# Splitting the 4-bit quantisation of one feed-forward block: eight chunks beside the first attention, three on GpSimd later

## What is computed

```python
x = x + tanh(g_xattn[0]) * L0_xattn(layernorm(x), ctx, ...)   # 32 heads of 128
x = x + tanh(g_ffn[0])   * L0_ffn(layernorm(x), 4-bit weights)
x = x + tanh(g_xattn[1]) * L1_xattn(...)
x = x + tanh(g_ffn[1])   * L1_ffn(...)     # base product + top-2 of 28 LoRA experts
x = x + tanh(g_xattn[2]) * L2_xattn(...)   # one head
x = x + tanh(g_ffn[2])   * L2_ffn(...)     # silu(x@dq1.T) * (x@dq2.T) @ dq3.T
x = x + tanh(g_xattn[3]) * L3_xattn(...)
x = x + tanh(g_ffn[3])   * L3_ffn(...)
```

```python
absmax = max(abs(block)); v = block / absmax
idx = searchsorted(bounds, v)          # 15 bounds, 16 code values
dq = CODE[idx] * absmax
```

## Time and profile before

| | us |
|---|---|
| median of 3 runs | 1882.26 |
| lowest, highest | 1872.6, 1884.25 |
| the profiled execution, its own time | 1874.59 |
| its span in the profile | 1872.9 |
| PE busy (share of the span) | 1460.5 (78%) |
| DVE busy | 1213.1 (65%) |
| ACT busy | 611.7 (33%) |
| POOL busy | 348.9 (19%) |
| mean granted PE clock | 0.889 |

### The profile page before, as it was taken

The page is one execution under the profiler, slowest core; times in us unless marked ns, Lnnn a source line. Parts: engine busy times, 40 slices in busy tenths (PEclk is TensorE's granted clock), DMA queues, the critical chain, the costliest instruction groups (busy, mean ns, idle before and its releaser), DMA issues.

```text
span 1872.9 us, 18291 instructions
## 1 busy us (share of the span) xinstructions
PE 1460.5 (78%) x6556; PEld 1020.8 (55%) x6556; DVE 1213.1 (65%) x1816; ACT 611.7 (33%) x912; POOL 348.9 (19%) x330
## 2 busy tenths in 40 slices
PE   7878778778746678578878888779999999997104
PEld 5545454445324545365746666557777777776101
DVE  4887888788885677542354444646666665667777
ACT  3544444444432233210121221134444344443003
POOL 1122132122213700010000000112212222123600
PEclk9998998989878799789569999989999999998556
DMA  5675776665572000002010112101101111000001
GB/s 193 156 181 137 143 178 150 160 141 138 117 136 99 34 11 1 0 23 68 0 34 17 46 38 77 48 9 57 57 23 39 53 57 57 1 1 1 0 0 45
DMA packets 37183, 127.69 MB, mean 68 GB/s; under 512 B 4288, under 2 KB 10304, under 8 KB 30896
## 3 DMA queue, kind: packets, MB, share of 16 engines
q1 hardware_dynamic: 26224, 83.38, 13.1%
q0 software_dynamic: 10880, 43.26, 13.0%
HBM read 72.63 MB, written 10.75 MB: 45 GB/s over the span
## 4 chain that ended last, share of the span: by engine, by line
PE 58%; DVE 20%; issue 10%; DVEq 5%; ACT 3%; POOL 1%; POOLq 1%; DMA 1%; SPq 0%
PE PS L151 10%; PE PS L153 9%; PE PS L152 9%; PE PS L492 6%; PE PS L467 4%; PE PS L825 3%; PE PS L861 3%; DVE AR L610 3%; DVE AR L2082 2%; DVEq L320 2%; DVE AR L631 2%; PE PS L451 2%; DVE AR L2076 2%; DVE AR L2080 1%; PE PS L847 1%
## 5 line engine op out<-in xcount | busy, mean ns | idle before, releaser
L492 PE MATMUL PS<-R,PT 128*128 128x512 f32 x256 | 158.0, 775 | 130.3 <-DVE X L646 130.3
L492 PEld LDWEIGHTS PS<-R,PT 128*128 128x128 f32 x256 | 61.5, 252 | 215.8 <-issue 215.8
L152 PE MATMUL PS<-R16r 128*128 128x512 f32 (+1 forms) x328 | 122.9, 375 | 0.0
L153 PE MATMUL PS<-R16r 128*128 128x512 f32 (+1 forms) x312 | 121.2, 388 | 0.0
L467 PE MATMUL PS<-R,HT 128*128 128x256 f32 x512 | 115.9, 379 | 0.0
L400 POOL DMA_DIRECT2D AR<-AR x40 | 49.6, 1240 | 307.7 <-DMA AR<-AR 239.4
L467 PEld LDWEIGHTS PS<-R,HT 128*128 128x128 f32 x512 | 94.8, 190 | 11.6
L151 PE MATMUL PS<-R16r,HTr 128*128 128x512 f32 (+1 forms) x224 | 91.3, 408 | 6.1 <-DVE X L1218 4.6
L151 PE MATMUL PS<-HTr,R16r 128*128 128x512 f32 (+1 forms) x240 | 90.4, 377 | 3.1 <-DVE R16r L193 1.6
L610 DVE SCALAR_TENSOR_TENSOR AR<-OT,AR 128x2112 f32<-128x2112 bf16 x32 | 75.5, 2359 | 21.8 <-ACT OT L555 19.4
L153 PE MATMUL PS<-HTr,R16r 128*128 128x512 f32 (+1 forms) x240 | 88.3, 368 | 0.0
(11 more groups left out here) (284 smaller groups left out, 3702.8 us busy)
## 6 DMA issues: line engine op xcount, KB each, us to landing
AR<-AR POOLq DMA_DIRECT2D x40, 1056.0 KB, 8.2
OR<-in_wo SPq DMA_DIRECT2D x12, 1024.0 KB, 5.0
dequantised<-AR SPq DMA_DIRECT2D x8, 1056.0 KB, 4.5
WR<-in_w0q SPq DMA_DIRECT2D x8, 1024.0 KB, 5.9
AR<-in_w3q SPq DMA_DIRECT2D x8, 1024.0 KB, 4.9
WR<-dequantised SPq DMA_DIRECT2D x22, 256.0 KB, 2.8
AR<-in_nf SPq DMA_DIRECT2D x4, 1056.0 KB, 6.0
nf_in<-in_nf SPq DMA_DIRECT2D x4, 1056.0 KB, 5.9
```

Source lines behind the costliest of these rows:

```text
L152: nc.tensor.matmul(out, ah, bl, start=False, stop=False)
L153: return nc.tensor.matmul(out, al, bh, start=False, stop=last_)
L492: i = nc.tensor.matmul(bank(5 + tt), PT[:, at:at + P], vo[:, pr, b, :], start=pr == 0, stop=pr == 1)
```

## The change

The chunks are cut anew. There are now eleven chunks of 128 x 1536 (`NF` = 11), one per slice of 128 hidden units, and the blocks of w3 are reordered so that slice f of stage f2 needs chunks up to f+1. Eight chunks stay beside stage x0, one per group as before, with the same instructions on 1536 columns. POOL's sum of `nf_above` and `nf_below` there becomes one more accumulating transfer (`join`), and the multiplication by the block maxima (`rescale`) is issued by POOL after the first accumulation of the next group. `nf_below`, `nf_above` and `absmax` have a buffer more. A chunk is stored by five transfers (six for chunk 0, seven for chunk 10) in place of one.

The last three chunks (8, 9, 10) are loaded once a1 is through with the buffers. DVE takes their maxima and normalises them in `dve_late`, between norm 3 and the gating of f1. POOL then computes all 15 steps of each: for each step it does one comparison with a multiplication (`tensor_scalar`) and, from the second on, one sum (`tensor_tensor`), both with a drain behind, and at the end the multiplication by the maxima and the stores, issued by POOL. Of the 45 steps five come after the gating (`h_ready`), twelve between norm 4 and norm 5, and 28 behind norm 5. The loads of slices 7, 8 and 9 in stage f2 wait for chunks 8, 9 and 10. A few semaphores of f3 are merged.

```diff
-NBU = NF * D // QB // NG
-NBT = 3 * NBU
+NBT = 3 * D // QB
+NARENA = 11616
@@ stores
+        def store_chunk(queue, k, src, signal):
+            queue.dma_start(scratch[:, 0:2, k * D:(k + 1) * D], src[:, 0:2 * D].rearrange("p (w n) -> p w n", w=2))\
+                .then_inc(signal, 16)
+            for at, b, n in w3_runs(k):
+                queue.dma_start(scratch[:, 2, b * QB:(b + n) * QB], src[:, 2 * D + at * QB:2 * D + (at + n) * QB])\
+                    .then_inc(signal, 16)
@@ pool_x0
-                nc.gpsimd.tensor_tensor(nf_result(g), nf_below, nf_above, ALU.add)
-                pool.drain().then_inc(A0["nf_free"], 1)
+                nc.gpsimd.dma_start(nf_below(g), nf_above(g), accum_op=ALU.add, max_dma_last_dim=4 * N_NF // 2)\
+                    .then_inc(A0["nf_joined"], 16)
+
+            def rescale(g):
+                pool.wait_ge(A0["nf_joined"], 16 * (g + 1))
...
+            for g in range(NG):
+                accumulate(g, 1)
+                if g:
+                    rescale(g - 1)
+                for k in range(2, NDOWN):
+                    accumulate(g, k)
+                join(g)
+            rescale(NG - 1)
@@ stage f1
+        def dve_late(dve):
+            dve.wait_ge(A0["nf_in"], 16 * ((NF + 1) // 2))
+            dve.wait_ge(A0["nf_in_odd"], 16 * (NF // 2))
+            for i, k in enumerate(LATE):
+                v = late_in(i).rearrange("p (n q) -> p n q", q=QB)
+                nc.vector.tensor_reduce(absmax[:, k], v, AX.X, ALU.max, apply_absolute_value=True)
...
+                nc.vector.tensor_tensor(v, v, rabs[:].unsqueeze(2).to_broadcast([P, NBT, QB]), ALU.mult)\
+                    .then_inc(A0["nf_v"], 1)
+                dve.drain()
+        STEPS = [(ALU.is_gt, b, r) for b, r in UP] + [(ALU.is_le, b, r) for b, r in DOWN]
+
+        def pool_late(pool, lo, hi):
+            for n in range(lo, hi):
...
+                if at == 0:
+                    pool.wait_ge(A0["nf_v"], k + 1)
+                    nc.gpsimd.tensor_scalar(late_sum(i), late_in(i), bound, step, op, ALU.mult)
+                    continue
+                nc.gpsimd.tensor_scalar(nf_in1[:], late_in(i), bound, step, op, ALU.mult)
+                pool.drain()
+                nc.gpsimd.tensor_tensor(late_sum(i), late_sum(i), nf_in1[:], ALU.add)
+                pool.drain()
+                if at == len(STEPS) - 1:
+                    v = late_sum(i).rearrange("p (n q) -> p n q", q=QB)
+                    nc.gpsimd.tensor_tensor(v, v, absmax[:, k].unsqueeze(2).to_broadcast([P, NBT, QB]), ALU.mult)
...
+                    store_chunk(nc.gpsimd, k, late_sum(i), A0["nf_late"])
@@ pool_f1, dve_f1
             pool_norm(pool, 3)
+            pool.wait_ge(F1["h_ready"], 1)
+            pool_late(pool, 0, 5)
...
             dve_norm(dve, 3, PAIRS - 1)
+            dve_late(dve)
             dve.wait_ge(F1["lg_ready"], T)
@@ sp_f2
+            for f in range(6, NF):
+                if 7 <= f < NF - 1:
+                    sp.wait_ge(A0["nf_late"], late(f + 1))
+                sp.wait_ge(F2["t_mm"], f * 3 - 3)
+                load(f, f % 2)
@@ POOL's program
             pool_norm(pool, 4)
+            pool_late(pool, 5, 17)
             pool_norm(pool, 5)
+            pool_late(pool, 17, len(LATE) * len(STEPS))
             pool_x3(pool)
```

More of the change, by code:

```diff
@@ L55, with down_blocks, w3_runs, stores @@
 FAR = 2.0 ** 100
+def down_blocks():
+    rows = [[2 * f, 2 * f + 1, 22 + 2 * f, 23 + 2 * f, 43 + 2 * f, 44 + 2 * f, 65 + 2 * f, 66 + 2 * f]
+            for f in range(NF - 1)]
+    last = NF - 1
+    return [21, 64] + [b for r in rows for b in r] + [2 * last, 22 + 2 * last, 43 + 2 * last, 65 + 2 * last, NB3, NB3 + 1]
+W3_BLOCKS = down_blocks()
+W3_PER = D // QB
+def w3_runs(k):
+    runs = []
+    for at, b in enumerate(W3_BLOCKS[k * W3_PER:(k + 1) * W3_PER]):
+        if runs and runs[-1][1] + runs[-1][2] == b:
+            runs[-1][2] += 1
+        else:
+            runs.append([at, b, 1])
+    return runs
+def stores(k):
+    return 1 + len(w3_runs(k))
 LOWEST = float(np.nextafter(np.float32(DOWN[-1][0]), np.float32(1.0)))
@@ L274, in build @@
         N_NF = NBT * QB
-        nf_in0, nf_below, nf_m0, nf_m1, nf_above = (AR[:, k * N_NF:(k + 1) * N_NF] for k in range(5))
+        nf_in0, nf_m0, nf_m1 = (AR[:, k * N_NF:(k + 1) * N_NF] for k in range(3))
         nf_in1 = sb("nf_in1", [P, N_NF])
@@ L298, in nf_mask, with stored_sem, stored @@
             return nf_m1 if n % 2 else nf_m0
-        def nf_result(g):
-            return nf_mask((g + 1) * (NDOWN - 1))
+        def store_chunk(queue, k, src, signal):
[4 more added lines that the diff above has]
+                    .then_inc(signal, 16)
+        def stored_sem(g):
+            return A0["nf_stored_odd" if g % 2 else "nf_stored"]
+        def stored(g):
+            return 16 * sum(stores(k) for k in range(g % 2, g + 1, 2))
         def pool_low(hi, lo, raw):
@@ L627, in down @@
                         dve.wait_ge(A0["nf_acc"], 16 * (n - 2))
[L628 to L629 removed]
                 bound, fall = DOWN[k]
[L631 removed]
+                nc.vector.tensor_scalar(nf_mask(n) if k else nf_below(g), nf_in(g), bound, fall, ALU.is_le, ALU.mult)\
                     .then_inc(A0["nf_mask"], 1)
@@ L1447, in tk, with late, late_in, late_sum @@
             return TK[:, i * T * NE:(i + 1) * T * NE]
+        LATE = range(NG, NF)
+        def late(k):
+            return 16 * sum(stores(j) for j in range(NG, k + 1))
+        def late_in(i):
+            return AR[:, 4096 + i * N_NF:4096 + (i + 1) * N_NF]
+        def late_sum(i):
+            return AR[:, 8704:8704 + N_NF] if i == 0 else late_in(i - 1)
+        def sp_late(sp):
+            sp.wait_ge(A1["pv_mm"], NU)
+            for i, k in enumerate(LATE):
+                sp.dma_start(late_in(i), nf_d[k]).then_inc(A0["nf_in_odd" if k % 2 else "nf_in"], 16)
@@ L1684, in sp_f2 @@
             load(1, 1)
-            with sp.Fori(0, 4) as k:
+            with sp.Fori(0, 2) as k:
                 for par in range(2):
```

100 lines of the change are left out of this document (54 added, 46 removed).

## The result

| | before | after |
|---|---|---|
| median, us | 1877.43 (1872.31 to 1884.25, 4 runs) | 1975.57 (1972.92 to 1979.26, 4 runs) |
| span of the profiled execution, us | 1872.9 | 1973.0 |
| POOL busy, us | 348.9 (19%) | 714.4 (36%) |

The ratio is 1.0522, interval [1.0475, 1.0568]: 5.2% slower, 98 us. The forecast was 1848, faster, and the time lies above the end of the range (1884). The function bodies have moved: the first late step is L1535, the others are L1537 (comparison) and L1539 (add), the late rescale is L1543; L631 became L676, L646 L691, L492 L541, L199 L224, L231 L256, L1812 L1920.

What follows compares the result with a forecast made beforehand. No engine is full; in x0 DVE and PE hand over to each other, so stages were priced singly. 57 - 1.4 - 3 - 2 - 6 - 11 = 34 off 1874.59 gives 1841, plus 7.7 is 1848; range 1814 to 1884.

Steps and rivals of the forecast that it cites:

- POOL's step: Late chunks: comparison 1.45, add 3.42, two drains of 0.15, so 5.2 us a step, bounds 5.1 and 7.1.
- (d): Late POOL comparison costs a two-input instruction or more; x is extra us per step; 1902 at 3.42, 1950 at 4.7; chance 0.12.
- Rival (b): Late POOL comparison costs twice the memset's rate, 2.7 us, giving 1874; chance 0.25 together with another rival.
- Port waits and norm 5: a2 and f2: 2 us lost in a2, 6 by norm 5 being late, 11 by L1812 waiting in eight slices.
- The store issues: Late chunks' stores issued by POOL: 1.24 us each, five 6.2, twelve 15.
- POOL's chain behind norm 5: f2: the 28 last steps with rescales and issues take 157 us, 167 with waiting for DVE.
- Scaling before the gating: f1: `dve_late` takes 12.9 us where DVE idles 10.6; with a little for the clock, 3 us lost.
- x0: Stage x0: groups take 58.0 us in place of 65.15, 57 us gained over eight groups.
- 0.3 for a remaining collision with `rescale`: x0, unit b0 of each group: `rescale`, some 8 us into the group, costs 0.3 us.
- The rule: DVE: a two-input SBUF or fast one-input instruction waits until POOL's running one ends; 2.2 and 3.4 us lost each group.
- the removed add: x0: POOL's sum of two chunks, L408, holds up DVE's L323, which takes 2.85 us where 0.6 was expected.
- to norm 1: x0's end: join landed after about 7.6 us, then 2.7, against 9.0 before; 1.4 us lost.

Runs made afterwards that it cites:

- experiment 1: Changed kernel with eleven other POOL instructions in turn beside the late comparison in steps 1 to 12; ran once, only single-instruction durations taken.
- experiment 2: Changed kernel with each of the 42 comparisons into the temporary replaced by a memset of the same 1536 columns: 1852.59 us.
- 3: Changed kernel without the 45 POOL steps of chunks 8 to 10, only rescale and stores kept: 1838.84 us.
- experiment 7: Kernel with no late steps, x0's two sums joined by POOL's add again in place of the accumulating transfer: 1811.81 us.
- experiment 10: Kernel with no late steps and the join by transfer, rescale issued after the second accumulating transfer of the next group: 1815.2 us.
- experiment 8: Changed kernel, each late comparison replaced by two arithmetic POOL instructions, steep line then clip, always min before max: 1890.57 us.
- experiment 5: Changed kernel with late ramps on ACT and sums on DVE in place of POOL's steps, third late chunk's scaling moved to a2: 1840.08 us.
- 9: Changed kernel with late chunks on ACT and DVE and x0's join by POOL's add again, whole result computed: 1815.1 us.

## Why the prediction failed, step by step

**POOL's step: the term that failed.** It was taken as 1.45 + 3.42 + 0.3 = 5.2, bounds 5.1 and 7.1. The add was right (3.44 to 3.46). The comparison was 5.38, above the upper bound as well. The bound rested on a premise, that one input and one output can't cost more than two inputs and one output, and on rows of other operations (a memset, an add). Neither excludes a dearer instruction: the trace of before held no long `tensor_scalar` on POOL at all, and experiment 1 shows that its price depends on its two operations by a factor of 3.7. The rival with the right mechanism was (d): its formula, a loss of 12x + 26x - 22, gives 127 us with x = 5.38 - 1.45 = 3.93, and so 1975; measured were 1975.6. That it fits to a us is partly luck: the kernel with the forecast's price takes 1852.6 and not 1848, and the dear comparison adds 123 and not 127. (d) got 0.12, and "all one-stream rows are near 0.9 ns per column" was the argument against it, a rule made from copies of one case. Rival (b), the comparison at 2.7 us, was too cheap by half as well (and twice the memset's 1.42 would have been 2.8). The Trainium skill (GPSIMD Engine Reference, Performance pitfalls for Q7 kernels) states 2.03 cycles per element for a body of compare and select that isn't unrolled. The prediction set that beside (b); the instruction here took twice (b)'s price. The Trainium skill (GPSIMD Engine Reference, Engine selection) calls one-input work roughly line-rate; here that holds for a copy, a memset and some pairs of operations (1.47 us), not for one operation alone (4.1) or for the comparison with its factor (5.38).

**Where the loss lands.** As the formula had it. Ahead of norm 5: 12 x 3.93 = 47; the waits of L224 for POOL are 67.3 us, 44 more than in experiment 2 (23.3); one of the twelve, L1535 of chunk 9, is dear in both, and 11 x 3.93 = 43. In f2: 26 x 3.93 - 22 = 80; from norm 5's last pair to the last L1920 the changed kernel takes 318.6 us and experiment 2 237.7, 81 more, of which 73 lie between the L1920 of slices 9 and 10, where PE waits 69.4 for slice 9's load, and 5 in the slices ahead of it.

**Port waits and norm 5.** Forecast 2 + 6 + 11 = 19; experiment 2 less 3 gives 13.8 by the medians and 17 by the traces from norm 4 on. L1920 takes 2.0 us in the mean of its first eight slices there, and the forecast's 2.5 was 0.5 too high: only the first three wait (2.34, 3.18 and 4.02), and in three of the later ones L1920 starts 0.05 us before POOL's add, which then waits itself (4.5 in place of 3.5). The store issues were mis-sized too, at 1.24 us each: five take 3.0 us (954.06 to 957.08 in the changed kernel), not 6.2. POOL's chain behind norm 5 takes 161 us in experiment 2, with one comparison in it left at 5.4, for 167.

With the dear comparison L1920's mean over all eleven slices is 2.4 (1.85 in experiment 2), and single instructions of DVE wait for nearly a whole POOL instruction (first the line's own durations, min, median and max in ns, with its first and last start; then DVE's timeline in a2):

```profile
L1920 DVE TENSOR_TENSOR R16r<-s_sb,R16r x11: 1217/2229/4385, 1002.3 to 1297.8; 128x1024 fp32r<-128x1024 f32 x11
```

```profile
860.79 4.41 DVE L224 TENSOR_SCALAR HN<-X,mv,rstd 128x512 f32<-128x512 f32 x1 [1.67 <-PE PS L280]
```

**Scaling before the gating.** Three chunks took 770.09 to 783.26, 13.2 us, for 12.9, and the first gating instruction came without idle time, as forecast. It starts 21.0 us after norm 3's last pair, where it started 18.1 after it before the change: 2.8 later, for 3. At norm 4's last pair 4.2 us are lost; no experiment isolates the 1.4 between.

**x0: right sum for the chunks, wrong for the join.** Forecast: 58.0 a group, 57 us in all. With the rescale out of DVE's way the groups take (503.7 - 98.4) / 7 = 57.9 with the add (experiment 7) and (503.5 - 99.1) / 7 = 57.8 with the transfer (experiment 10), and the last join starts 63 us earlier than before (566.8 to 503.7). As built they take 60.7 and the gain is 44. That the sum is met to 0.1 us does not show each of its unit terms. The failed term is "0.3 for a remaining collision with `rescale`", which was 3 a group. The rule (a two-input or fast DVE instruction waits for POOL's running one) was in the prediction's first part, and the time of the rescale ("some 8 us into the group") too; what was not done was to lay that time on DVE's timeline and see which instruction it meets. That the removed add would give back its 2.2 us was true only of 2112 columns: at 1536 it ends before it does harm (0.9 us).

**The sum again.** The forecast was made for the profiled execution, 1841, and 7.7 us were added because that execution (1874.59) is below the median of its runs. The kernel before scatters from 1872 to 1885 us, the changed one from 1973 to 1979 and experiment 2 from 1852 to 1854, with the profiled execution within 1 us of the median in both (1852.92 for 1852.59 in experiment 2). So like has to be compared with like: 1841 forecast, 1852.9 measured at the forecast's price of a step. That 1848 lies so near to 1852.6 is luck. Timelines of POOL and DVE, first of the kernel before, then of experiment 2 (the last join, the last pair of norms 1, 3, 4 and 5, the last `low_act` of f2; norms 4 and 5 of before are in the earlier trace rows):

```profile
566.85 4.64 POOL L408 TENSOR_TENSOR AR<-AR 128x2112 f32<-128x2112 f32 x1 [10.64 <-DVE AR L610]
586.22 0.42 POOL L229 TENSOR_SCALAR veps<-mv 128x2 f32<-128x2 f32 x1 [2.35 <-DVE mv L174]
806.06 0.42 POOL L229 TENSOR_SCALAR veps<-mv 128x2 f32<-128x2 f32 x1 [3.50 <-DVE mv L174]
...
1197.27 2.23 DVE L1812 TENSOR_TENSOR R16r<-s_sb,R16r 128x1024 fp32r<-128x1024 f32 x1
```

```profile
523.82 1.19 POOL L445 DMA_DIRECT2D AR<-AR  x1 [9.31 <-DVE AR L657]
546.21 0.42 POOL L254 TENSOR_SCALAR veps<-mv 128x2 f32<-128x2 f32 x1 [2.35 <-DVE mv L199]
763.68 0.42 POOL L254 TENSOR_SCALAR veps<-mv 128x2 f32<-128x2 f32 x1 [3.49 <-DVE mv L199]
859.34 0.42 POOL L254 TENSOR_SCALAR veps<-mv 128x2 f32<-128x2 f32 x1 [28.79 <-DVE mv L199]
936.22 0.42 POOL L254 TENSOR_SCALAR veps<-mv 128x2 f32<-128x2 f32 x1 [3.29 <-DVE mv L199]
...
1173.91 2.24 DVE L1920 TENSOR_TENSOR R16r<-s_sb,R16r 128x1024 fp32r<-128x1024 f32 x1
```

| stretch | forecast, us | before less experiment 2, us |
|---|---|---|
| x0, to the last join | +57 | +43.0 |
| to norm 1 | -1.4 | -3.0 |
| to norm 3 (a1) | 0 | +2.4 |
| to norm 4 (f1) | -3 | -4.2 |
| to norm 5 (a2) | -8 | -7.5 |
| to the last `low_act` (f2) | -11 | -7.3 |
| to the end | 0 | -1.7 |
| sum | 34 | 21.7 |

So next to POOL's price the join's term in x0 is the one that failed, by 14 us; the others are off by 0.5 to 3.7 us each, in both directions. Up to 4 of the 7.5 before norm 5 are chunk 9's first comparison, left at 5.4 us. The dear comparison takes a further 123.

## To carry to other kernels

Price an operation that the trace doesn't show by its own measurement, or keep the range open upwards: rows of other operations are no upper bound for it. When a long chain is put on a helper engine, write the end time as slope times the price of its step; here one us of POOL's step was worth up to 38 us (85 us for 2.24 from experiment 8 to the changed kernel), and that slope should set the weight of the rival. When a transfer takes the place of an instruction, look where the instruction behind it now starts, and what it meets there.

## What the runs showed of the hardware

- A POOL `tensor_scalar` on 128x1536 f32 takes 1.47 us with `mult, add` or with `min, max`, 4.1 us with one operation alone (`mult`, `add` or `is_gt`), and 5.38 us with `is_gt` or `is_le` and `mult`, or 5.37 with `max, min`. A copy or a memset takes 1.47, a two-input add, subtraction or product 3.44. Which further pairs are fast is open; so is why.
- DVE is held up by a running POOL instruction, but not always until that one ends. L224 (one long input, 0.54 us alone) ended some 0.3 us behind POOL's, comparison, add or memset, and took up to 5.0. L1920 (two inputs in SBUF, 1.22 alone) ended 1.1 us behind a running add, but 0.2 us before the end of a running comparison (six cases in the changed kernel; POOL 1036.63 for 5.38 us, L1920 1038.75 for 3.03), took up to 4.4, and did not wait for a memset at all. POOL is held up in turn: an add of its that started 0.05 us behind L1920 took 4.5 in place of 3.5.
- Spreading 45 DVE and 42 ACT instructions over the waits of f1, a2 and f2 cost 1.2 us (experiment 5 against 3) and 3.3 us (9 against 7), some 2.4 us that the moved scaling gave back already taken off.
